# Projecting keys and values of one group of the 64-wide heads two layers earlier

## The reference, cut to what matters

```python
# layer 1, experts: each expert takes its 64 best tokens of a batch
Sm = jnp.swapaxes(jax.nn.softmax(logits, axis=-1), 1, 2)
G, I = jax.lax.top_k(Sm, K)                      # K = 64 of the tokens
# layer 2: 16 heads of 8, then each token takes 2 of 8 gated experts
# layer 3, attention: 16 heads of 64, causal
qh = (q @ Wq.T + bq).reshape(b, s, H, HD).transpose(0, 2, 1, 3)
kh = (k @ Wk.T + bk).reshape(b, s, H, HD).transpose(0, 2, 1, 3)
vh = (v @ Wv.T + bv).reshape(b, s, H, HD).transpose(0, 2, 1, 3)
scores = jnp.einsum('bhqd,bhkd->bhqk', qh, kh) / np.sqrt(HD)
```

## Time and profile before

| | us |
|---|---|
| median of 3 runs (lowest, highest) | 1885.74 (1882.33, 1887.26) |
| the profiled execution's own time | 1887.47 |
| its span in the trace | 1885.7 |
| TensorE busy | 1685.3 (89%) |
| VectorE, ScalarE, GpSimd busy | 1077.8, 907.8, 652.8 |
| DMA read, written | 34.46 MB, 28.65 MB |

### The profile page before, as it was taken

How to read it: one execution, slowest core, us unless ns; L and a number is a source line. 1 busy time by engine, 2 the same in 40 slices (tenths; PEclk the granted TensorE clock), 3 DMA queues, 4 the chain that set the end, 5 groups by cost and what they waited for, 6 DMA issues and landing times.

```text
span 1885.7 us, 50612 instructions
## 1 busy us (share of the span) xinstructions
PE 1685.3 (89%) x19910; PEld 1238.5 (66%) x19910; DVE 1077.8 (57%) x3127; ACT 907.8 (48%) x2468; POOL 652.8 (35%) x651
## 2 busy tenths in 40 slices
PE   6999974897689999997999975999899999999878
PEld 3666663676458878884666654999476666666753
DVE  5788656687432222215667864666466666565558
ACT  3444411685344444442434323777665555565525
POOL 3333203585311111103315445555243333333315
PEclk8999966887589999997999987999999999999969
DMA  5000000000000000005521011222300000000001
GB/s 184 15 14 9 3 1 27 18 13 1 7 1 2 1 2 1 1 1 209 218 76 61 23 38 56 70 63 56 101 13 18 1 18 18 7 1 1 1 1 45
DMA packets 50053, 65.85 MB, mean 35 GB/s; under 512 B 8810, under 2 KB 38405, under 8 KB 49565
## 3 DMA queue, kind: packets, MB, share of 16 engines
q1 hardware_dynamic: 45469, 54.14, 8.8%
q0 software_dynamic: 4352, 8.47, 1.4%
HBM read 34.46 MB, written 28.65 MB: 33 GB/s over the span
## 4 chain that ended last, share of the span: by engine, by line
PE 59%; DVE 8%; issue 7%; POOL 4%; POOLq 3%; DVEq 2%; ACT 1%; DMA 1%; SPq 1%; PEldq 0%; PEld 0%; ACTq 0%
PE single L1918 6%; PE quad L1906 5%; PE quad L2256 2%; PE quad L2262 2%; PE single L2273 2%; PE pair L2662 2%; PE pair L1879 2%; PE single L2688 2%; PE quad L2697 2%; PE single L2674 2%; PE quad L2636 2%; PE quad L2674 1%; PE single L2697 1%; PE quad L2662 1%; PE pair L1962 1%
## 5 line engine op out<-in xcount | busy, mean ns | idle before, releaser
L2887 POOL TENSOR_TENSOR arena<-arena 128x512 f32<-128x512 f32 x128 | 130.4, 1040 | 285.4 <-DVE arena L2817 285.4
L284 POOL TENSOR_TENSOR rstd<-var_eps,neg_half 128x4 f32<-128x4 f32 (+1 forms) x64 | 66.1, 1032 | 297.9 <-DVE var_eps L280 251.7
L1991 ACT ACTIVATE arena<-quad,arena 128x256 f32<-128x256 f32 x256 | 110.7, 475 | 98.6 <-PE quad L1906 98.5
L972 POOL TENSOR_SCALAR arena<-arena 128x512 f32<-128x512 f32 x56 | 86.9, 1567 | 174.9 <-ACT arena L769 171.1
L2082 DVE TENSOR_TENSOR arena<-single,arena 128x512 f32<-128x512 f32 x32 | 22.1, 692 | 206.8 <-PE single L1918 206.8
L847 DVE TENSOR_REDUCE arena<-quad 128x8 f32<-128x1024 f32 x86 | 104.6, 1218 | 55.3 <-PE pair L656 29.7
L2754 ACT ACTIVATE arena<-pair,arena 128x128 f32<-128x128 f32 x256 | 90.9, 380 | 80.5 <-DVE arena L2812 80.5
L2754 ACT ACTIVATE arena<-quad,arena 128x128 f32<-128x128 f32 x256 | 90.9, 382 | 79.5 <-DVE arena L2812 79.5
L817 ACT ACTIVATE arena<-quad 128x1024 f32<-128x1024 f32 x86 | 86.3, 1023 | 82.2 <-PE quad L684 42.8
L1906 PE MATMUL quad<-arena,wide 128*128 128x256 f32 x512 | 121.8, 385 | 3.0 <-issue 2.1
L1918 PE MATMUL single<-wide,arena 128*64 128x128 f32 x2048 | 123.9, 275 | 0.0
(11 more groups left out here) (527 smaller groups left out, 4446.7 us busy)
## 6 DMA issues: line engine op xcount, KB each, us to landing
tokens_by_expert<-arena SPq DMA_DIRECT2D x22, 780.0 KB, 8.2
arena<-in_ctxT SPq DMA_DIRECT2D x32, 256.0 KB, 3.0
arena<-tokens_by_expert SPq DMA_DIRECT2D x72, 65.0 KB, 1.8
wide<-in_w SPq DMA_DIRECT2D x2, 2048.0 KB, 11.2
arena<-outputs_by_choice SPq DMA_DIRECT2D x16, 256.0 KB, 3.8
wide<-in_wgu SPq DMA_DIRECT2D x1, 2736.0 KB
x<-in_x SPq DMA_DIRECT2D x4, 512.0 KB, 7.3
out_x<-x SPq DMA_DIRECT2D x8, 256.0 KB, 2.3
```

The lines of the kernel that those rows point to most:

```text
L972: mm = pool.tensor_scalar(kv[g % 2][:, :, a, :], kf[g % 2], kmask[:, a:a + 1], None, ALU.mult)
L1991: act.activation(h1T[e % 4][:, f, :], bank[2 + f][:, 0:G * K], ACT.Gelu_apprx_tanh, bias=b1c[:, e, f:f + 1]).then_inc(s["h_evac"], 1)
L2887: pool.tensor_tensor(part, part, inv[t % 3][:, 4 * r:4 * r + 4].unsqueeze(2).broadcast_to([P, 4, P]), ALU.mult).then_inc(s["norm_ready"], 1)
```

## The change

Keys and values of the third group (`CHOICE_GROUP` = 2) are projected in the opening of `expert_choice`: 16 pieces in two PSUM banks (3 and 7), copied by ScalarE to `choice_stage`, stored by SP to `kv_store` in device memory. In `wide_heads` the group's slots keep only the query products, and SP reads keys and values back: keys once scores(7) are done, values once attend(7) is done, both ahead of the results and the context of group 3. The wait for `fw_in[1]` moves behind the selection's transposition. The weights, biases and the context block for the pieces are loaded in `linear_attention`. Of group 0's 16 pieces, six (`TAIL`) move from the gated opening to the end of `small_heads(2)`: one ahead of `output(NG - 1)`, five behind it, ahead of the barrier. `first_kT` and `first_v` change places in SBUF.

```diff
@@ -317,25 +317,54 @@
         FILL, FILLS = 12, (E * REGION + E * P) // (12 * P)
         UNIT = 2 * G
         AHEAD = 2
+        TAIL = 6
...
-        first_kT = arena.fixed(KV_AT, [HB, W])
-        first_v = arena.fixed(KV_AT + 4096, [G, H * 64])
+        first_v = arena.fixed(KV_AT, [G, H * 64])
+        first_kT = arena.fixed(KV_AT + 4096, [HB, W])
...
-        EARLY = 6
+        CHOICE_GROUP = 2
+        kv_store = nc.dram_tensor("keys_values_ahead", [1, 2 * HB, P, W], F32).ap()
+        choice_stage = ([arena.fixed(20544 + i * W, [W]) for i in range(8)] +
+                        [arena.fixed(EARLY_END + i * W, [W]) for i in range(8)])
...
-            "early_mm", "early_kept", "wo_early", "wq_early", "cols_early", "cvec_mm3", "cvec_ready3")
+            "early_mm", "early_kept", "wo_early", "wq_early", "cols_early", "cvec_mm3", "cvec_ready3",
+            "staged", "k_back", "v_back")
+
+        def early_piece(pe, i, dst, ctx, done):
+
+            if i < HB:
+                mm = pe.matmul(dst, early_wk[:, i * P:(i + 1) * P], ctx, start=True, stop=True)
+            else:
+                j, a = divmod(i - HB, 2)
+                mm = pe.matmul(dst, ctx[:, j * P:(j + 1) * P], early_wv[:, a * 512:(a + 1) * 512],
+                               start=True, stop=True)
+            mm.then_inc(done, 1)
+
+        def keep_piece(act, i, dst, src, done):
+
+            if i < HB:
+                mm = act.activation(dst, src, ACT.Identity, bias=bcol[:, 1, i:i + 1])
+            else:
+                mm = act.activation(dst, src, ACT.Copy)
+            mm.then_inc(done, 1)
+
+        def first_place(i):
+            if i < HB:
+                return first_kT[:, i, :]
+            j, a = divmod(i - HB, 2)
+            return first_v[:, j, a * 512:(a + 1) * 512]
...
@@ -564,13 +593,8 @@
                 for g in range(2, NG):
                     load_ctx(sp, g)
                     if l == 2 and g == 6:
-                        sp.dma_start(early_wk, t["wk3"]).then_inc(early_in, 16)
-                        sp.dma_start(early_wv, t["wv3"]).then_inc(early_in, 16)
                         for i in range(2):
                             sp.dma_start(wide_ctx[i], t["ctxT"][:, i * W:(i + 1) * W]).then_inc(early_in, 16)
-                        sp.dma_start(bcol[:, 0:3, :], t["bqkv3"]).then_inc(early_in, 16)
-                        sp.dma_start(bo3, t["bo3"].rearrange("(a n) -> a n", a=1).broadcast_to([P, P])
-                                     ).then_inc(early_in, 16)
                     if l == 2 and g < 6:
                         if g == 2:
                             sp.wait_ge(blanked, 1)
...
@@ -758,7 +782,16 @@
                         project_k(g + 2, m_take(pe, ("k", g + 2)))
                 sum_values(N - 1)
                 sum_ones(N - 1)
+                if l == 2:
+                    w = twin_sems("pipelines", WIDE_SIGNALS)
+                    pe.wait_ge(early_in, 16 * 7)
+                    early_piece(pe, 0, bank[2], wide_ctx[0], w["early_mm"])
                 output(NG - 1)
+                if l == 2:
+                    for i in range(1, TAIL):
+                        if i >= 3:
+                            pe.wait_ge(w["early_kept"], i - 2)
+                        early_piece(pe, i, bank[2 + i % 3], wide_ctx[0], w["early_mm"])
                 barrier(pe, phase)
 
             def scalar(act):
...
@@ -828,6 +861,12 @@
                         evac_v(g + 1, M[:])
                     if j == 3 and g + 2 < NG:
                         evac_k(g + 2, M[:])
+                if l == 2:
+                    w = twin_sems("pipelines", WIDE_SIGNALS)
+                    act.wait_ge(early_in, 16 * 7)
+                    for i in range(TAIL):
+                        act.wait_ge(w["early_mm"], i + 1)
+                        keep_piece(act, i, first_place(i), bank[2 + i % 3], w["early_kept"])
                 barrier(act, phase)
 
             def vector(dve):
...
@@ -1415,6 +1454,14 @@
                 sp.dma_start(em, t["mask1"]).then_inc(ww_in, 16)
                 for g in range(1, NG):
                     contexts(g)
+                    if g == 4:
+                        sp.dma_start(early_wk, t["wk3"]).then_inc(early_in, 16)
+                        sp.dma_start(early_wv, t["wv3"]).then_inc(early_in, 16)
+                        sp.dma_start(wide_ctx[0], t["ctxT"][:, CHOICE_GROUP * W:(CHOICE_GROUP + 1) * W]
+                                     ).then_inc(early_in, 16)
+                        sp.dma_start(bcol[:, 0:3, :], t["bqkv3"]).then_inc(early_in, 16)
+                        sp.dma_start(bo3, t["bo3"].rearrange("(a n) -> a n", a=1).broadcast_to([P, P])
+                                     ).then_inc(early_in, 16)
                 barrier(sp, phase)
 
             def tensor(pe):
...
@@ -1865,6 +1913,10 @@
                 for e in range(E):
                     row = t["b2_1"][e].rearrange("(a n) -> a n", a=1)
                     sp.dma_start(b2p[K * (e % 2):K * (e % 2) + K, e // 2, :], row.broadcast_to([K, P])).then_inc(fw_in[1], 16)
+                for i in range(2 * HB):
+                    sp.wait_ge(s["stage_kept"], i + 1)
+                    sp.dma_start(kv_store[0, i], choice_stage[i]).then_inc(s["staged"], 16)
+                sp.wait_ge(s["staged"], 16 * 2 * HB)
                 barrier(sp, phase)
 
             def tensor(pe):
...
@@ -1886,19 +1938,32 @@
                                           weighted[j % 2][:, 2 * k:2 * k + 2, :].rearrange("p e k -> p (e k)"), ident[:])
                     mm.then_inc(s["pt_ready"], 1)
 
-                pe.wait_ge(fw_in[1], 16 * fw_loads[1])
+                def early(pieces):
+                    for i in pieces:
+                        if i >= 2:
+                            pe.wait_ge(s["stage_kept"], i - 1)
+                        early_piece(pe, i, bank[3 + 4 * (i % 2)], wide_ctx[0], s["stage_mm"])
+
+                pe.wait_ge(early_in, 16 * 5)
+                early(range(0, 3))
                 pe.wait_ge(s["gates_ready"], 1)
                 for k in range(2):
                     mm = pe.transpose(bank[4][:, k * P:(k + 1) * P],
                                       gate_of[:, 16 * k:16 * k + 16, :].rearrange("p b e -> p (b e)"), ident[:])
                 mm.then_inc(s["gT_ready"], 1)
+                early(range(3, 11))
                 pe.wait_ge(s["sel_ready"], 1)
                 pe.transpose(bank[5][:, 0:P], sel[:, 0, :], ident[:]).then_inc(s["selT_ready"], 1)
 
+                pe.wait_ge(fw_in[1], 16 * fw_loads[1])
                 pe.wait_ge(s["selT_copied"], 1)
                 pe.matmul(bank[6][:, 0:P], upper, selT[:, 0, :], start=True, stop=True).then_inc(s["pos_ready"], 1)
+                early(range(11, 14))
                 for j in range(G):
                     prep(0, 0, j, first=True)
+                    if j < 2:
+                        early((14 + j,))
+                pe.wait_ge(s["stage_kept"], 2 * HB)
 
                 def first(g, u, e):
                     for f in range(FB):
...
@@ -1972,6 +2037,14 @@
                 act.activation(gate_of.rearrange("p b e -> p (b e)"), lg.rearrange("p b e -> p (b e)"),
                                ACT.Exp).then_inc(s["exp_ready"], 1)
 
+                def keep_early(pieces):
+                    for i in pieces:
+                        act.wait_ge(s["stage_mm"], i + 1)
+                        keep_piece(act, i, choice_stage[i], bank[3 + 4 * (i % 2)], s["stage_kept"])
+
+                act.wait_ge(early_in, 16 * 5)
+                keep_early(range(0, 14))
+
                 def prep(g, u, j):
                     act.wait_ge(s["ga_ready"], G * g + j + 1)
                     act.activation(exT[u][:, :, j * K:(j + 1) * K], bank[0][:].rearrange("p (e k) -> p e k", e=E),
@@ -1979,8 +2052,11 @@
                     act.wait_ge(s["pt_ready"], G * g + j + 1)
                     act.activation(weightedT[u][:, j, :, :].rearrange("p e k -> p (e k)"), bank[1][:],
                                    ACT.Copy).then_inc(s["pt_evac"], 1)
+                act.wait_ge(fw_in[1], 16 * fw_loads[1])
                 for j in range(G):
                     prep(0, 0, j)
+                    if j < 2:
+                        keep_early((14 + j,))
                 act.drain().then_inc(s["h_evac"], FB)
 
                 def group(g, u, last):
...
@@ -2198,25 +2274,17 @@
                 def early(pieces):
 
                     for i in pieces:
-                        if i >= 3:
+                        if i >= TAIL + 3:
...
+                        early_piece(pe, i, early_bank[i % 3], wide_ctx[0], w["early_mm"])
+
+                early(range(TAIL, 8))
                 for g in range(2):
...
-                early(range(3, 4))
+                early(range(8, 9))
                 for g in range(2):
...
-                early(range(4, 9))
+                early(range(9, 14))
                 pe.wait_ge(s["sel_ready"], 1)
```

(38 more changed lines are left out.)

23 lines of the change are left out of this document (3 added, 20 removed).

## The result

The changed kernel takes 1856.27 us (median of 4 runs, 1853.98 to 1864.42) against 1886.5 us for the kernel before beside it: ratio 0.9851, 95% interval 0.9815 to 0.9887, or about 28 us less. A repeat gave 0.9867 (0.9845 to 0.9888). The forecast was 1868.0, with about 1863.6 as its low end (1865.6, and 2 us for the spread): right in direction, but the kernel gained 10 us more than the 17.7 that were forecast.

The account below looks back on a forecast made before the run. TensorE was taken as the busy engine, so its idle places and those where it alone sets the pace matter. −14.9 − 2.5 − 0.3 = −17.7 us gave 1869.8 profiled, 1868.0 as median; low end 1865.6 and 2 us for spread, high end 1877.

Parts of the forecast that it names:

- Part 1: Wide heads' second group: sixteen key and value products leave slots 8 to 15, −14.9 us, bounds −13.6 and −15.4.
- first rival: Wide heads' second group stops being bound by TensorE, gives 9.8 to 10.9 us, total 1872 to 1873; chance 0.17.
- Part 2: Expert choice's opening: sixteen products enter, the wait for bias rows ahead of the gates goes; −2.5 us, bounds −4.3 and +1.
- second rival: Clock stays low in the choice's opening: pieces take 1.9 us, +14 us, total about 1884.5; chance 0.05.
- the rule of the Trainium skill: Choice's opening: matmuls cycling through PSUM banks with short idles can swing between two clocks, making the step +14 us.
- Part 3: End of the 8-wide heads: six products ahead of the barrier are hidden, 0 us, upper bound +3.5.
- Part 4: Gated opening with ten products instead of sixteen: −0.3 us, bounds 0 and −0.4; other products lie under TensorE's 15.75 us wait.
- Part 5: Wide heads: SP reads keys and values back before group 3's results; 0 us, 2 us to spare, +4 at half rate.
- a sign of being wrong: Wide heads, slot 10: VectorE waiting for `outputs_by_choice` would show the forecast wrong.
- The sum: Whole kernel: −14.9 − 2.5 − 0.3 = −17.7 us, giving 1868.0 as median of the runs.

Follow-up runs that it names:

- experiment 2: Changed kernel with all sixteen pieces of group 0 back behind the barrier, none ahead of it: 1855.48 us, ratio 0.9855.
- Experiment 7: Kernel before with 33 more TensorE instructions (66 waits already met) ahead of the expert choice's loop: 1878.72 us, ratio 0.9955.
- Experiment 3: Changed kernel with the wide heads' second group projecting its own keys and values again, nothing read back; pieces and stores stay: 1872.87 us, ratio 0.9938.
- the 64 no-operations: Kernel before with 64 no-operations written for TensorE in the choice's opening, which add one instruction to the built program: 1882.25 us, ratio 1.0004.
- experiment 5: Kernel before with only the wait for the bias rows moved behind the selection's transposition: 1880.92 us, ratio 0.9988.
- experiment 6: Kernel before with only the tail, six pieces of group 0 moved ahead of the barrier: 1883.13 us, ratio 1.0.
- 6 to 10: Includes: before with 33 instructions behind the choice's loop, 0.9976; after with 128 more waiting instructions, 0.9913; after with one piece ahead of the gates' transposition, 0.986.
- the 192 no-operations: Kernel after with 192 no-operations written for TensorE in linear attention, which add no instruction to the built program: 1853.26 us, ratio 0.9849.

## Why the prediction was right, and where it wasn't

**Part 1, the sixteen products** (−14.9): 58.88 − 44.56 = 14.3 us where the results are in time, 13.8 in the profile after. Held, by 0.6 to 1.1 us less than forecast. The first rival (results late, or VectorE's stall in all four pairs) didn't come.

**Part 2, the opening** (−2.5): −2.47 us, each step within 0.6 us. The transposition comes 5.4 us after SP's first issue instead of the forecast's 4.9 (512.0 − 507.13); from there to the selection's it is 8.03 us, so nothing was lost where 0.3 was given; the eight pieces come 0.96 us apart (two every 1.9 us) against the forecast's 0.93, and the clock rises beside them: in the timeline above the pieces' first row has 2.05 us, the gathers' 1.12. The low clock that the second rival wanted, and with it the rule of the Trainium skill, "TensorE: Matmul & The Clock Gate", that the prediction names, isn't seen: the pieces do cycle through two banks, and once the clock is up they take 1.02 to 1.18 us each to the end.

**Part 3** (0): held; experiment 2 gives the same time without the tail, and the copies end ahead of the barrier, which GpSimd opens.

**Part 4, the gated opening** (−0.3): the gap in GpSimd's scatters closed, 0.63 to 0.30 us, as forecast. The stage is 1.3 us shorter in the first pair of profiles, and repeats only within 0.7. Over all of them it takes 40.5 to 41.3 us in the seven kernels' profiles with the tail (40.69 with the tail alone) and 41.1 to 41.9 in the seven without it (41.40 for the changed kernel without it). So some 0.8 us here are the tail's, a term that the forecast left out: the other products there do not all lie under the wait.

**Part 5, the way back** (0, 2 us to spare): nearly. Timelines of SP and of VectorE after:
```profile
1392.17 3.02 SPq L2682 DMA_DIRECT2D arena<-keys_values_ahead  x4
1395.23 1.02 SPq L2650 DMA_DIRECT2D arena<-outputs_by_choice  x2
...
1397.88 2.48 SPq L2650 DMA_DIRECT2D arena<-outputs_by_choice  x1
```
```profile
1404.68 2.36 DVE L2659 SCALAR_TENSOR_TENSOR x<-arena,choice_w,x 128x128 f32<-128x128 f32 x8 [0.42 <-DMA arena<-outputs_by_choice]
```
VectorE waited 0.42 us for the results, which the prediction had named as a sign of being wrong: the spare time was gone. In the repeat it didn't wait. The size is 0.5 us (45.06 against 44.56).

**The sum** (−14.9 − 2.5 − 0.3) is the step that failed. It adds up the stretches that the edits touch and takes every other stretch as it was. A term is missing: what the change's 65 more instructions of TensorE ahead of the loop do by moving the code behind them. Experiment 7 shows such a shift alone, with none of the change's work: 8.5 us (5.3 to 11.9) for 33 instructions. The change's own 65 were not run alone; that they are worth about as much is argued from the signs that both kernels share (no second fetch, fifth group 40.12 us, landing 2.1 us, no pause of 2.1 us). With it the sum is −14.3 − 2.5 − 8.5 = −25.3, and some 0.8 us of the gated opening, which leaves 2 us of 28, inside the intervals. Experiment 3 bears it out: 2.5 + 8.5 + 0.8 = 11.8 against the 11.7 us that it kept. The kernel before shows three places where it was to be had:

*The loop's second pass.* 42.65 or 44.04 us against 40.12: 2.5 to 3.9 us.

*A pause in the 8-wide heads.* In all five profiles of the kernel before and its variants without the 33 instructions (before, its repeat, the 64 no-operations, experiments 5 and 6) TensorE stands still for 2.1 us at one instruction (L656 in the kernel before), again on nothing that the profile shows. The first row is the repeat's timeline; the two after it are its DMA queues over that pause (932.2 to 934.6 us):
```profile
934.48 1.14 PE L656 MATMUL quad<-arena 32*128 32x512 f32 x8 [2.10 <-issue]
```
```profile
q1 hardware_dynamic: 171, 0.96, 100.4%
q8 instruction: 1, 0.02, 2.5%
```
The instruction packet stands among the packets of a load that keeps the DMA engines full. After the pause the clock drops; windows of the same profile, before the pause and after it:
```profile
921.50:933.50 12.00, 10.88 (x278) 7.24 (x277) 6.92 (x15) 6.42 (x9) 3.95 (x3) 1.00 0.88 346
936.00:943.00 7.00, 7.00 (x86) 4.67 (x78) 4.35 (x10) 0.79 (x2) 0.00 (x0) 0.51 0.02 9
```
TensorE busy all of 7 us at a clock of 0.51, the lower of its two levels (1.2 of 2.4 GHz), costs some 3.5 us more. But the drop doesn't always follow. Experiment 6 has the same pause, at 939.01 us, and this window after it:
```profile
940.00:947.00 7.00, 7.00 (x167) 4.80 (x163) 5.08 (x11) 2.90 (x4) 0.27 (x1) 1.00 0.07 23
```
In the three profiles with pause and drop the 8-wide heads take 265.90 to 267.58 us, in the two with the pause alone (experiments 5 and 6) 263.10 and 263.00. The two kernels with the 33 instructions, ahead of the loop or behind it, have no such pause of over 0.9 us and take 263.06 and 262.09. So the pause hangs on the placement, and most of what the stage lost in the profiles is the clock's, which differs from execution to execution. The kernel after had in one profile a pause of 1.10 us and in the repeat none (264.99 and 258.67).

*The last scatter.* The chain of waits, first of the kernel before (the repeat), then of the kernel after:
```profile
1318.89 3.92 DMA outputs_by_choice<-arena
```
```profile
1317.13 2.09 DMA outputs_by_choice<-arena
```
And the DMA queues over these landings (1318.8 to 1321.8, and 1317 to 1320 us):
```profile
q8 instruction: 1, 0.02, 2.4%
q0 software_dynamic: 64, 0.00, 1.6%
```
```profile
q0 software_dynamic: 64, 0.00, 1.6%
```
The scatter's 64 packets are the same; in the kernel before an instruction packet of 16 KB lies among them, and the landing takes 1.8 us longer. Over the scatters into `outputs_by_choice` of all fourteen profiles whose landing the traces have, the 220 without a packet of q8 take 2.26 us in the median and the 86 with one 2.72, up to 5.93. A packet need not lengthen a landing: that of experiment 6 (2.11 us) has one at its very end. Everything behind it waits: TensorE idles 2.43 to 2.55 us at the wide heads' first transposition in place of 0.74, its next products take 2.04 in place of 1.10, and the opening is 1.6 us longer. In all profiles that land in about 2.1 us (after, its repeat, experiments 2, 3, 6 to 10, and the 192 no-operations) the wide opening takes 29.1 to 29.3 us, in those that land in 3.9 to 4.2 (before, its repeat, the 64 no-operations, experiment 5) 30.5 to 30.9.

Stage by stage, experiment 7 against the profile of before gives: fifth group −2.5, 8-wide heads −2.9, gated stages −2.3, wide opening −1.8, slots 0 to 7 −0.5, and +1.0 in the choice's opening: −9.1, against the 8.5 of the timed runs. Two of these terms are the clock's and not the placement's: the 8-wide heads' (above), and the opening's, where the waits delay the transposition by 0.14 us and the rest comes with the second gather at the low clock; the repeat of the kernel before has an opening 0.9 us longer without any waits. The stages ahead of the edit, 5.6 us shorter in this profile, are left out.

What stays open: where in the program the boundaries lie, so that one could say beforehand which shift helps; what the change's own shift of 65 is worth alone; why experiment 6, which has the short landing and a wide opening shorter by 1.8 us, measures no gain; and the last 2 us of the 28. Taking away the load that stands beside the pause was not tried.

## What to carry to other kernels

An edit moves all code behind it. Where one engine's program is long and unrolled, or has a loop, look before the forecast at the instruction queue's packets and at idle time of the busiest engine whose releaser is "issue": such pauses can come or go with an edit, whatever it is for, and here a shift of 33 instructions was worth half as much as the forecast of the whole edit. Before crediting a gain to an edit, run the kernel before with the same number of idle instructions at the same place, and count both in the built program: the no-operations written here left next to none, and a product that is one line of the kernel was four instructions. And price those instructions: 128 of them cost 9 us where the engine was idle for only 4.

## What the runs showed that was not expected

A loop of TensorE was fetched again on its second pass in one placement (8 packets of instructions, 1.9 to 2.1 us without work at the jump) and not in three others. With one instruction packet of 16 KB among its 64 small ones the last scatter landed after 3.9 to 4.2 us in place of 2.1. A pause of 2.1 us of a busy TensorE was followed by 7 to 10 us at the lower clock in three profiles of five, and by none in two. And with 128 instructions that only wait, each on two semaphores long met, TensorE was idle for 13.11 us in place of 4.36, some 0.1 us for each.
